# A top-2 expert kernel on one core: the first delta product put earlier, a sort step moved from TensorE to VectorE, integer packing moved later

## The reference

```python
# x (16,128,128) f32, cond (16,8): weights of LoRA experts AND router logits
x = x + (x @ W_base.T + b_base + 2 * sum_e cond[b,e] * ((x @ As[e].T) @ Bs[e].T))
rw = softmax(cond); w, sel = top_k(rw, 2); w = w / w.sum()      # then w/12 + (1-1/12)*w
mlp(x, g, u, d) = (gelu_tanh(x @ g) * (x @ u)) @ d              # 128 -> 512 -> 128
x = x + sum over the 2 chosen experts of w * mlp(x, expert) + mlp(x, shared)
```

## Time and profile before

| | us |
|---|---|
| median of 3 runs (130.94 to 131.41) | 131.17 |
| the profiled execution, its own time | 130.85 |
| its span, first to last instruction | 129.2 |
| TensorE busy | 124.9 (97%) |
| VectorE busy | 90.2 (70%) |
| ScalarE busy | 72.0 (56%) |
| GpSimd busy | 61.8 (48%) |

### The profile page before, as it was taken

The page is one execution under the profiler, slowest core; times in us unless marked ns, Lnnn a source line. Parts: engine busy times, 40 slices in busy tenths (PEclk is TensorE's granted clock), DMA queues, the critical chain, the costliest instruction groups (busy, mean ns, idle before and its releaser), DMA issues.

```text
span 129.2 us, 3167 instructions
## 1 busy us (share of the span) xinstructions
PE 124.9 (97%) x873; PEld 113.9 (88%) x873; DVE 90.2 (70%) x177; ACT 72.0 (56%) x136; POOL 61.8 (48%) x111
## 2 busy tenths in 40 slices
PE   6999999999999999999999999999999999999991
PEld 5948887878887888998999999999999999999990
DVE  1686798769979999633377768667867686766731
ACT  2349677976956877113466485648565846711110
POOL 5364974463797877453344632643364604610000
PEclk9999999999999999999999999999999999999999
DMA  2998778799100077679745686558699960014922
GB/s 39 266 329 313 218 272 219 296 310 292 36 3 0 5 173 239 233 275 411 302 183 223 244 322 231 208 223 325 228 315 306 402 211 0 3 26 141 263 82 61
DMA packets 14524, 26.56 MB, mean 206 GB/s; under 512 B 2224, under 2 KB 7600, under 8 KB 12976
## 3 DMA queue, kind: packets, MB, share of 16 engines
q1 hardware_dynamic: 14048, 26.28, 60.8%
q10 hardware_dynamic: 464, 0.13, 0.4%
HBM read 12.52 MB, written 1.31 MB: 107 GB/s over the span
## 4 chain that ended last, share of the span: by engine, by line
PE 97%; issue 0%; DVE 0%; DVEq 0%
PE bank L1059 11%; PE bank L1100 9%; PE bank L1101 9%; PE bank L1099 9%; PE bank L1081 6%; PE bank L1004 6%; PE bank L1005 6%; PE bank L1006 6%; PE bank L1121 5%; PE bank L1122 4%; PE bank L1123 4%; PE bank L1022 3%; PE bank L928 3%; PE bank L936 3%; PE bank L1023 3%; PE bank L1024 3%
## 5 line engine op out<-in xcount | busy, mean ns | idle before, releaser
L558 ACT ACTIVATE work<-bank 128x512 f32<-128x512 f32 x48 | 28.7, 599 | 38.3 <-PE bank L1101 17.6
L720 DVE TENSOR_TENSOR bank<-bank,work 128x512 f32<-128x512 f32 x40 | 27.9, 698 | 18.3 <-PE bank L1101 13.1
L739 DVE TENSOR_TENSOR hT_lo<-bank,hT_hi 128x512 fp32r<-128x512 f32 x40 | 27.3, 682 | 1.0 <-issue 0.5
L1099 PE MATMUL bank<-xp,wst 128*128 128x256 f32 x96 | 27.2, 284 | 0.0
L1101 PE MATMUL bank<-xp,wst 128*128 128x256 f32 x96 | 27.2, 283 | 0.0
L1100 PE MATMUL bank<-xp,wst 128*128 128x256 f32 x96 | 27.2, 283 | 0.0
L485 POOL TENSOR_TENSOR wstd<-wexd,wstd 128x512 fp32r<-128x512 f32 x12 | 15.6, 1296 | 24.0 <-ACT wstd L600 24.0
L567 ACT CAST hT_hi<-bank 128x512 fp32r<-128x512 f32 x40 | 23.3, 583 | 1.8 <-DVE bank L720 1.8
L1099 PEld LDWEIGHTS bank<-xp,wst 128*128 128x128 f32 x96 | 18.4, 192 | 0.0
L1100 PEld LDWEIGHTS bank<-xp,wst 128*128 128x128 f32 x96 | 18.4, 192 | 0.0
L1101 PEld LDWEIGHTS bank<-xp,wst 128*128 128x128 f32 x96 | 18.4, 192 | 0.0
(11 more groups left out here) (156 smaller groups left out, 214.0 us busy)
## 6 DMA issues: line engine op xcount, KB each, us to landing
wst<-wex SPq DMA_DIRECT2D x12, 1024.0 KB, 5.0
raw_ex<-n_L_cond_skill_gate_dram SPq DMA_DIRECT2D x8, 256.0 KB, 3.5
raw_ex<-in_L_cond_skill_up_dram SPq DMA_DIRECT2D x8, 256.0 KB, 4.1
sst<-n_L_cond_skill_gate_dram SPq DMA_DIRECT2D x8, 256.0 KB, 3.5
sst<-in_L_cond_skill_up_dram SPq DMA_DIRECT2D x8, 256.0 KB, 4.0
xn<-in_x_dram SPq DMA_DIRECT2D x4, 256.0 KB, 4.8
out_dram<-xT SPq DMA_DIRECT2D x4, 256.0 KB, 2.7
sst<-_L_cond_shared_gate_dram SPq DMA_DIRECT2D x1, 256.0 KB, 4.9
```

Source lines behind the costliest of these rows:

```text
L558: act.activation(gelu_sb[q], gate_ps[q][:, :], ACT.Gelu_apprx_tanh).then_inc(gelu_done, 1)
L720: dve.tensor_tensor(up_ps[u][:, :], up_ps[u][:, :], gelu_sb[q], ALU.mult).then_inc(h_done, 1)
L739: dve.tensor_tensor(hT_lo[:, q, :], up_ps[u][:, :], f32(hT_hi[:, q, :]), ALU.subtract).then_inc(lo_done, 1)
L1099: pe.matmul(of_c, w_hi, x_hi, start=True, stop=False)
```

## The change

- One warm-up product fewer (7 to 6), and of the remaining ones none between cond's and B's transposes, two after B's. The first `delta_w` comes ahead of x's first transposes, the second ahead of the counts. The second `x_transposes` waits for the first of the set-up copies instead of the third.
- ScalarE copies the counts after the first copy of x and the gelu table's load instead of ahead of them. VectorE computes the router's weights after `w_eff(1)` instead of before and after `w_eff(0)`.
- `sort_starts` and ScalarE's copy of its result go. The operands of the second count product are swapped, so that every batch's row holds all experts' n. VectorE computes twos and remainders of the eight experts (three operations, after `gated` of chunk 0), multiplies them with a constant mask `below` and sums over the experts in front (after `gated` of chunk 1). GpSimd's steps from there are one or two fewer.
- `two_e` and `four_e` are packed in group 3 as before; `two_b`, `slot_eb` and `four_b` after the last `sum_group`, `six_b` after `gated_single(1)`.

```diff
-    WARM_UP = (4, 2, 1)
+    WARM_UP = (4, 2)
...
-            pool.memset(upick[:, :, :], 2.0).then_inc(const_fill, 1)
+            pool.memset(below[:, 0, :, :], 2.0).then_inc(const_fill, 1)
+            pool.memset(below[:, 1, :, :], 1.0).then_inc(const_fill, 1)
...
+            for i in range(2):
+                pool.affine_select(out=below[:, i, :, :], in_=below[:, i, :, :], compare_op=ALU.is_gt, fill=0.0,
+                                   base=0, pattern=[[1, 9], [-1, 8]], channel_multiplier=0).then_inc(consts, 1)
...
-            pool.wait_ge(sort_sum, 2)
-            pool.tensor_scalar(par[:, :], half[:, :], -2.0, None, ALU.mult).then_inc(sort_step, 1)
-            pool.wait_ge(sort_step, 4)
-            pool.tensor_tensor(par[:, :], par[:, :], rank_n[:, 1, :], ALU.add).then_inc(sort_step, 1)
-            pool.wait_ge(sort_sb, 2)
-            pool.tensor_tensor(pos_e[:, 0, :], rank_n[:, 0, 0:8], starts[:, 2, :], ALU.subtract).then_inc(sort_step, 1)
-            pool.tensor_tensor(pos_e[:, 1, :], rank_n[:, 0, 0:8], starts[:, 0, :], ALU.add).then_inc(sort_step, 1)
+            pool.wait_ge(sort_sum, 5)
+            pool.tensor_tensor(pos_e[:, 1, :], rank_n[:, 0, 0:8], starts[:, 0, 0:8], ALU.add).then_inc(sort_step, 1)
+            pool.tensor_scalar(pos_e[:, 2, :], starts[:, 1, 0:8], starts[:, 0, 8:9], None, ALU.add).then_inc(sort_step, 1)
+            pool.wait_ge(sort_step, 5)
+            pool.tensor_tensor(pos_e[:, 2, :], pos_e[:, 2, :], pos_e[:, 1, :], ALU.subtract).then_inc(sort_step, 1)
             pool.wait_ge(sort_step, 6)
-            pool.tensor_scalar(pos_e[:, 0, :], pos_e[:, 0, :], 0.0, None, ALU.is_equal).then_inc(sort_step, 1)
+            pool.wait_ge(sort_sum, 6)
+            pool.tensor_tensor(pos_e[:, 2, :], pos_e[:, 0, :], pos_e[:, 2, :], ALU.mult).then_inc(sort_step, 1)
+            pool.wait_ge(sort_step, 7)
+            pool.tensor_tensor(pos_e[:, 3, :], pos_e[:, 1, :], pos_e[:, 2, :], ALU.add).then_inc(sort_step, 1)
             pool.wait_ge(sort_step, 8)
-            pool.tensor_tensor(pos_e[:, 2, :], pos_e[:, 0, :], starts[:, 1, :], ALU.mult).then_inc(sort_step, 1)
-            pool.wait_ge(sort_step, 9)
-            pool.tensor_tensor(pos_e[:, 3, :], pos_e[:, 1, :], pos_e[:, 2, :], ALU.add).then_inc(sort_step, 1)
-            pool.wait_ge(sort_step, 10)
...
-            act.wait_ge(sort_mm, 1)
-            act.copy(rank_n[:, :, :], count_ps[0:B, 0:2 * B].rearrange("p (a b) -> p a b", a=2)).then_inc(sort_sb, 1)
             copy_xT(0)
             act.wait_ge(exp_done, 1)
             act.activation(rt[:, 24:25], rt[:, 8:9], ACT.Gelu_apprx_tanh).then_inc(gelu_table, 1)
+            act.wait_ge(sort_mm, 1)
+            act.copy(rank_n[:, :, :], count_ps[0:B, 0:2 * B].rearrange("p (a b) -> p a b", a=2)).then_inc(sort_sb, 1)
             copy_xT(1)
...
-                    if g == 0 and c == 2:
-                        act.wait_ge(sort_mm, 2)
-                        act.copy(starts[:, :, :], start_ps[0:B, 0:24].rearrange("p (a b) -> p a b", a=3)
-                                 ).then_inc(sort_sb, 1)
...
             scale_B(1)
-            router_weights()
             dve.wait_ge(setup_ps, 3)
             dve.wait_ge(consts, 1)
             dve.tensor_tensor(wT[:, :], bank[6][:, 0:H], ident[:, :], ALU.add).then_inc(setup_sb, 1)
             dve.wait_ge(setup_sb, 3)
             w_eff(0)
+            w_eff(1)
+            router_weights()
             router_sum()
-            w_eff(1)
             w_eff(2)
...
-                        dve.wait_ge(consts, 8)
+                        dve.wait_ge(consts, 7)
                         dve.wait_ge(sort_sb, 1)
-                        dve.tensor_tensor(n_ge[:, :, :],
-                                          rank_n[:, 1, :].rearrange("p (b a) -> p b a", a=1).to_broadcast([B, B, 8]),
-                                          thr[:, :].rearrange("p (a r) -> p a r", a=1).to_broadcast([B, B, 8]),
+                        n = rank_n[:, 1, 0:8]
+                        dve.tensor_tensor(n_ge, n.rearrange("p (e a) -> p e a", a=1).to_broadcast([B, 8, 8]),
+                                          thr[:, :].rearrange("p (a r) -> p a r", a=1).to_broadcast([B, 8, 8]),
                                           ALU.is_ge).then_inc(sort_sum, 1)
                         dve.wait_ge(sort_sum, 1)
-                        dve.tensor_reduce(half[:, :], n_ge[:, :, :], AXIS_X, ALU.add).then_inc(sort_sum, 1)
+                        dve.tensor_reduce(twos_odd[:, 0, :], n_ge, AXIS_X, ALU.add).then_inc(sort_sum, 1)
+                        dve.wait_ge(sort_sum, 2)
+                        dve.scalar_tensor_tensor(twos_odd[:, 1, :], twos_odd[:, 0, :], -2.0, n, ALU.mult, ALU.add
+                                                 ).then_inc(sort_sum, 1)
+                    if g == 0 and c == 1:
+                        dve.wait_ge(sort_sum, 3)
+                        dve.tensor_tensor(in_front, twos_odd[:, :, :].rearrange("p i (a e) -> p i a e", a=1)
+                                          .to_broadcast([B, 2, 9, 8]), below[:, :, :, :], ALU.mult).then_inc(sort_sum, 1)
+                        dve.wait_ge(sort_sum, 4)
+                        dve.tensor_reduce(starts[:, :, :], in_front, AXIS_X, ALU.add).then_inc(sort_sum, 1)
+                        dve.scalar_tensor_tensor(pos_e[:, 0, :], twos_odd[:, 0, :], 2.0, rank_n[:, 0, 0:8],
+                                                 ALU.mult, ALU.is_equal).then_inc(sort_sum, 1)
...
                         dve.tensor_copy(idx[:, :], list_ps[0:1, 0:64]).then_inc(lists_ready, 1)
+                    if g == 3 and c == 1:
                         dve.wait_ge(lists_ready, 2)
-                        dve.wait_ge(packs, P_PAD)
-                        pack(two_b[:, 1:17], idx[:, 32:64:2], B, idx[:, 33:64:2])
-                    if g == 3 and c == 1:
-                        dve.wait_ge(packs, P_TWO_B)
-                        pack(slot_eb[:, :], idx[:, 0:LEFT:2], B * B, two_b[:, 1:1 + NP])
                         pack(two_e[:, :], idx[:, LEFT:LEFT + NS:2], E, idx[:, LEFT + 1:LEFT + NS:2])
                     if g == 3 and c == 2:
                         dve.wait_ge(packs, P_TWO_E)
                         pack(four_e[:, :], two_e[:, 0:4:2], E * E, two_e[:, 1:4:2])
-                        pack(four_b[:, :], two_b[:, 1 + NP:17:2], B * B, two_b[:, 2 + NP:17:2])
-                    if g == 3 and c == 3:
-                        pack(six_b[:, :], two_b[:, 0:NP:3], B * B, two_b[:, 1:NP:3])
-                        dve.wait_ge(packs, P_SIX_PART)
-                        pack(six_b[:, :], six_b[:, :], B * B, two_b[:, 2:NP:3])
+            def pack_batches():
+                dve.wait_ge(packs, P_PAD)
+                pack(two_b[:, 1:17], idx[:, 32:64:2], B, idx[:, 33:64:2])
+                dve.wait_ge(packs, P_TWO_B)
+                pack(slot_eb[:, :], idx[:, 0:LEFT:2], B * B, two_b[:, 1:1 + NP])
+                pack(four_b[:, :], two_b[:, 1 + NP:17:2], B * B, two_b[:, 2 + NP:17:2])
+            def pack_slots():
+                pack(six_b[:, :], two_b[:, 0:NP:3], B * B, two_b[:, 1:NP:3])
+                dve.wait_ge(packs, P_SIX_PART)
+                pack(six_b[:, :], six_b[:, :], B * B, two_b[:, 2:NP:3])
...
             sum_group(NG - 1)
-            dve.wait_ge(packs, P_SIX_B)
+            pack_batches()
+            dve.wait_ge(packs, P_FOUR_B)
             first = of_four(read(dve, four_b, 0, B ** 4))
             gated_single(1)
+            pack_slots()
             add_single(0, first[0])
             gated_single(2)
...
             last = of_four(read(dve, four_b, 1, B ** 4))
+            dve.wait_ge(packs, P_SIX_B)
             dve.wait_ge(sum_done, NG)
             three_slots(0)
...
-            warm_up(WARM_UP[1])
             pe.wait_ge(ld_b, 16)
...
             def sort_counts():
-                pe.wait_ge(consts, 8)
+                pe.wait_ge(consts, 7)
                 pe.wait_ge(sort_step, S_MEMB)
                 pe.matmul(count_ps[0:B, 0:B], ltri[:, :], memb_sum[:, :], start=True, stop=True)
-                pe.matmul(count_ps[0:B, B:2 * B], memb_sum[:, :], ones[:, 0:B], start=True, stop=True).then_inc(sort_mm, 1)
-            def sort_starts():
-                pe.wait_ge(sort_sum, 2)
-                pe.wait_ge(sort_step, S_PAR)
-                pe.wait_ge(x1lo_ready, NG)
-                pe.matmul(start_ps[0:B, 0:24], half[:, :], upick[:, :, :].rearrange("p a e -> p (a e)"),
-                          start=True, stop=False)
-                pe.matmul(start_ps[0:B, 8:16], par[:, :], ltri[:, 0:8], start=False, stop=True).then_inc(sort_mm, 1)
+                pe.matmul(count_ps[0:B, B:2 * B], ones[:, 0:B], memb_sum[:, :], start=True, stop=True).then_inc(sort_mm, 1)
             def sort_singles():
...
-            warm_up(WARM_UP[2])
+            warm_up(WARM_UP[1])
+            pe.wait_ge(ld_a, 16)
+            delta_w(0)
             x_transposes(0)
             pe.wait_ge(ld_w, 16)
```

(33 more changed lines are left out.)

34 lines of the change are left out of this document (10 added, 24 removed).

## The result

Over five executions the changed kernel took 128.78, 129.40, 129.82, 130.89 and 131.39 us, median 129.82, and the kernel before, in as many beside it, 130.91 to 131.41, median 130.94. The ratio is 0.9874, interval 0.9854 to 0.9894; it leaves out executions more than 1.5% above the fastest of their kernel, here the two upper ones of the changed kernel, so it shows more than the means of all five do (130.06 against 131.07, a ratio of 0.992), and so do the ratios of experiments 1, 2, 9, 13 and 14. The kernel before scatters by 0.5 us, the changed one by 2.6, and that had to be explained.

What follows compares the result with a forecast made beforehand. The prediction took TensorE's queue, busy 97% of the span, as the bound. Terms of 0.07, 0.31 and 0.11 us summed to 0.49 off the 131.17 median, giving 130.7 us, range 130.1 to 131.5.

Steps and rivals of the forecast that it cites:

- Starts leave TensorE: Experts' starts: four 16-row passes and shape changes leave TensorE, 0.385 us, less 0.08 for a late load: 0.31 net.
- The late load at 22.0: Chunk 1's down product: its weight load waits for hT_lo behind VectorE's three new operations, giving back 0.08 us.
- Packs and `six_b`: Group 3's last chunk: without the six_b pair hT_lo starts 0.26 us earlier and the late load goes, 0.11 gained.
- Third rival: Singles: packs each wait for GpSimd, the second single's down product waits 1.3 us on TensorE; 132.0 us, chance 0.06.
- Second rival: After gated(1): three VectorE operations take a microsecond, hole 0.4 to 0.5, six_b's removal brings nothing; 131.1 to 131.2, chance 0.18.
- The first delta product's time: Head: the first delta product was to stream from 5.08 us, shown as a start near 5.0.
- Fourth rival: Head: the new hole delays the clock level's rise, costing 0.8 to 2.3 us; 131.5 to 133.0 us, chance 0.12.
- the same hole: Head: TensorE idle 0.29 us, from 4.79 to 5.08, ahead of the first delta product, waiting for the scaled B.
- the head's term: Head: one warm-up product fewer, mostly taken back by a hole, 0.07 us gained if the level rises when it did.
- The sum: Whole kernel: head 0.07, starts 0.31 and packing 0.11 together take 0.49 us off.

Runs made afterwards that it cites:

- 1: The changed kernel run again with no edit, beside the kernel before: 128.86 to 131.18 us, mean 0.63 below before, ratio 0.9888.
- 2: The kernel before with only the head's edits (warm-up, TensorE's order, ScalarE's copy, VectorE's router order): 129.42 to 131.84 us, mean 0.33 below before, ratio 0.9896.
- 9: The changed kernel with all seven packs put back into group 3, head and starts kept: 129.29 to 131.41 us, mean 0.58 below the kernel before, ratio 0.9948.
- 13: The changed kernel without its edit of the starts, head edits and moved packs kept: 129.24 to 131.55 us, mean 0.29 below the kernel before, ratio 0.9963.
- 14: The changed kernel unchanged, seven more executions beside the kernel before: 128.89 to 131.65 us, mean 0.36 below before, ratio 0.9908.
- the kernel before again: The kernel before run once more, unchanged: 130.06 to 130.76 us, ratio 0.9991.
- 11: The kernel before with only the experts' starts moved to VectorE, head and packs as before: mean 0.03 us above before, ratio 1.0003.
- (5, 2): The changed kernel with five instead of four warm-up products ahead of cond's transpose: 129.39 to 130.14 us, mean 1.12 below the kernel before, ratio 0.9915.
- (5, 3): The changed kernel with five warm-up products ahead of cond's transpose, three before the first delta product: 129.39 to 130.25 us, 1.09 below the kernel before, ratio 0.9918.
- (4, 0): The changed kernel without the two warm-up products ahead of the first delta product: 130.82 to 132.26 us, 0.62 above the kernel before, ratio 1.0050.
- the fourth run: The changed kernel unchanged, one further profiled execution: 131.26 us, with the clock's rise at 10.08.
- (6, 2): The changed kernel with eight warm-up products instead of six, six ahead of cond's transpose: 129.43 to 130.91 us, 0.48 below the kernel before, ratio 0.9966.

## Why the prediction was wrong

- **Starts leave TensorE (0.31): right.** To single 32.72 before, 32.40 to 32.44 after, 0.28 to 0.32. The late load at 22.0 that I had charged with 0.08 appeared as 0.06.
- **Packs and `six_b` (0.11): right in size where it stands, incomplete.** From first single to first slot 12.63 before and 12.42 to 12.50 after, 0.13 to 0.21. But the kernel before again took 12.48 with its packs in place, since its TensorE had waited for the single's weights and its last lo half was in time, so the term is there only where that wait is not. The larger part was missing: I had costed the packs' removal from group 3 by the stall in `slot_eb` and looked only at whether TensorE waited in that one execution. That `two_b` got in 0.02 us ahead of GpSimd stood in the trace, and I did not read it as a margin that other edits can use up. With packs in group 3 the other two edits lose 0.4 to 0.6 us to it (experiments 2, 9, 11).
- **Third rival, packs late at the singles: did not happen.** One of three waits. **Second rival, VectorE takes TensorE's place: not either**, the pass at 22.99 is 0.06 late and not 0.4. The Trainium skill ("SBUF — State Buffer", section "SBUF: two separate sides") says that whichever of a GpSimd operation and a VectorE operation with two inputs in memory, or in a mode that uses two ports, starts first keeps the port for its whole instruction. The trace agrees for `two_b` and its two inputs, 0.17 against 1.20; it also shows 0.82 us against 0.22 for the 16x2 router operation L645, which has one tensor input and a scalar column, and no row tells in which mode that one ran.
- **The first delta product's time: right** (5.13 against a forecast near 5.0). **Fourth rival, the level rises later:** its effect came in the profiled execution, 2.0 us later and 1.0 us lost, but not by its mechanism, since with (5, 2) the same hole stood and the rise was early.
- **The step that failed** is the head's term, 0.07, worked out in before's timeline with the rise left at 7.9. The rise moves from execution to execution even with the same kernel (7.89 and 6.61 before), and the changed head moves it both ways. By the ruler, 9 of the changed kernel's 19 executions rose between about 4.5 and 7 us (128.8 to 129.9) and 10 between about 8 and 10.5 (130.5 to 131.7). The late rises stand in profiles; the early ones of this kernel are worked out, and a profile shows one only with (5, 2) and (5, 3). I had the late side with a chance of 0.12 and no early side at all.
- **The sum, at equal rise, holds.** The two profiled executions differ by 2.03 us in the rise, 1.01 us at a half each; the changed one took 0.54 more, so 0.47 less at equal rise, where I had 0.49. The median of 129.82 came from three early executions in five, which was luck of the draw: the median over 19, 130.54, lies in the range.
- **A slip in the chances.** "Slower is the last two and a rest: 0.16" does not add up, since the last two rivals alone have 0.06 and 0.12.
- The Trainium skill ("TensorE: Matmul & The Clock Gate", section "What's actually happening") calls the moment of release run-variable and puts its cost under 1% of a typical kernel; the trace agrees in the first, with rises from 5.3 to 10.1 us, and not in the second: at half a microsecond each, that is 2.4 us or 1.8% of this kernel.

What stays open: what in the head decides between early and late. One more product ahead of cond's transpose made all of six executions early, two more ten of twelve, and (4, 0) left none below 130.8; one more elsewhere was tried only on top of this one, with (5, 3). The idle time ahead of cond's transpose does not order the rises: 0.17 us went with 10.08 in the fourth run, 0.24 with 7.01 in head and starts, which has the changed kernel's head.

Why `two_b` gets in ahead of GpSimd is open too. It does in both profiles of the kernel before, by 0.02 and 0.03 us, and in none of the five other kernels that pack in group 3. The traces show where the difference enters: VectorE's copy to `idx` starts 1.00 and 0.97 us behind GpSimd's subtraction in the two profiles of before and 1.15 to 1.36 behind it in the five others.

## To carry to other kernels

Ask of every short kernel when its clock level rises, and read several executions before costing anything ahead of that point. A warm-up product costs up to 0.4 us of TensorE at the low level; here one more narrowed the scatter from 2.3 to 0.75 us, and its gain of 0.5 us in the mean is not clear of noise. A tiny VectorE operation placed beside GpSimd's large ones takes 0.15 us or up to 1.2, by a few hundredths of a microsecond in their order: move it to where VectorE has time to spare, and count its loss in the stretches where VectorE's lead over TensorE is small. Edits of which each uses up the lead that the next one needs can measure nothing alone, so try them together.

## What was not expected of the hardware

- The rise of TensorE's clock from 1.2 to 2.4 GHz lay between 5.25 and 10.08 us by the records, and near 4.4 by the spacing of passes with (6, 2), in kernels that differ by one or two small products. The 19 times of the changed kernel fall in two groups with means of 129.2 and 131.1 us; head and packs, with the same head, shows no such gap in twelve.
- VectorE operations on 16 to 32 elements took 0.15 to 0.17 us or 0.97 to 1.23 us, by whether they started 0.02 to 0.03 us ahead of a large GpSimd operation or 0.07 to 0.35 behind its start. The slow ones ended within 0.03 us of GpSimd's operation.
- A stall on TensorE costs the stall and 0.11 us more for the late weight load behind it (0.335 to 0.341 instead of 0.227 between the next starts) in each of the five profiles that wait for VectorE's lo half at a down product of group 3.
